# A fused four-layer transformer kernel: row maxima transposed in one rounded pass, more idle products and new interleaving tables

## The reference

```
scores = jnp.where(causal, scores, NEG)
m = jnp.max(scores, axis=-1, keepdims=True)
e = jnp.exp(scores - m)
attn = e / jnp.sum(e, axis=-1, keepdims=True)
```

## Time and profile before

| | us |
|---|---|
| median of three runs | 3338.98 |
| the profiled execution | 3332.12 |
| its span, first to last instruction | 3330.2 |
| mean granted TensorE clock in it | 0.851 |

### The profile page before, as it was taken

One profiled execution on the slowest core, in us unless ns is written; L12 is line 12 of the kernel. 1 busy time (PEld: TensorE's weight loads), 2 busy tenths in 40 slices (PEclk: granted clock), 3 DMA queues, 4 the chain that ended last, 5 costly groups with the idle time before them and its releaser, 6 DMA issues.

```text
span 3330.2 us, 50269 instructions
## 1 busy us (share of the span) xinstructions
PE 2776.6 (83%) x20640; PEld 1752.4 (53%) x20640; DVE 1760.9 (53%) x2698; ACT 1912.7 (57%) x1963; POOL 3.6 (0%) x13
## 2 busy tenths in 40 slices
PE   7999989778997789977898888987889879897426
PEld 4776556454564545645455554555545545554213
DVE  5464464644656446564555545555455554564425
ACT  2333334875248753587535864468634686347996
POOL 0000000000000000000000000000000000000000
PEclk8998899779997688977999778987779887898558
DMA  3000000000000000000000000000000000000000
GB/s 128 2 1 1 19 2 1 1 1 7 1 1 1 0 8 1 1 1 1 8 2 1 1 1 8 2 1 1 1 4 2 1 1 1 4 1 1 0 0 7
DMA packets 4570, 18.83 MB, mean 6 GB/s; under 512 B 608, under 2 KB 864, under 8 KB 3808
## 3 DMA queue, kind: packets, MB, share of 16 engines
q1 hardware_dynamic: 4320, 15.38, 1.2%
HBM read 13.28 MB, written 2.10 MB: 5 GB/s over the span
## 4 chain that ended last, share of the span: by engine, by line
PE 58%; ACT 19%; DVE 12%; issue 11%; DVEq 0%; DMA 0%; ACTq 0%; SPq 0%
ACT back_cosines L1379 6%; PE two_ps L1934 3%; ACT back_cosines L1381 3%; PE one_ps L918 2%; PE one_ps L1934 2%; PE two_ps L1334 2%; PE one_ps L1220 2%; PE two_ps L966 1%; PE one_ps L1782 1%; PE two_ps L918 1%; ACT L1379 1%; PE one_ps L893 1%; PE two_ps L613 1%; PE one_ps L899 1%; PE one_ps L822 1%
## 5 line engine op out<-in xcount | busy, mean ns | idle before, releaser
L1379 ACT ACTIVATE back_cosines<-back_cosines 128x2048 f32<-128x2048 f32 x256 | 473.3, 1899 | 0.5
L989 ACT ACTIVATE front_scratch<-one_ps 128x1152 f32<-128x1152 f32 x168 | 171.6, 1022 | 230.4 <-PE one_ps L904 230.2
L1934 PEld LDWEIGHTS two_ps<-zero_f,wts 128*128 128x128 f32 x1270 | 210.1, 232 | 114.6 <-issue 90.9
L1934 PE MATMUL two_ps<-zero_f,wts 128*128 128x128 f32 x1270 | 235.2, 327 | 35.1 <-DVE back_cosines L1452 18.1
L1381 ACT ACTIVATE back_cosines<-back_cosines,wts 128x2048 f32<-128x2048 f32 x128 | 252.1, 1994 | 13.3 <-DVE back_cosines L1452 13.1
L853 DVE TENSOR_REDUCE front_negm<-one_ps 128x8 f32<-128x1024 f32 (+1 forms) x168 | 202.5, 1221 | 99.0 <-PE one_ps L828 97.7
L1389 DVE TENSOR_REDUCE back_nsum<-back_cosines 128x8 f32<-128x2048 f32 x64 | 144.4, 2281 | 186.9 <-ACT back_cosines L1379 186.9
L752 ACT ACTIVATE back_cosines<-two_ps,wts 128x512 fp32r<-128x512 f32 x28 | 19.2, 687 | 236.3 <-PE two_ps L966 236.3
L822 PE MATMUL one_ps<-front_qkr 32*128 32x128 f32 (+1 forms) x896 | 117.8, 363 | 42.7 <-issue 34.4
L1452 DVE TENSOR_SCALAR back_cosines<-two_ps 128x2048 f32<-128x2048 f32 x56 | 128.1, 2287 | 30.2 <-PE two_ps L1313 30.1
L989 ACT ACTIVATE back_cosines<-two_ps 128x1152 f32<-128x1152 f32 (+1 forms) x84 | 86.1, 1025 | 98.3 <-PE two_ps L904 98.3
(11 more groups left out here) (635 smaller groups left out, 5941.8 us busy)
## 6 DMA issues: line engine op xcount, KB each, us to landing
wts<-w_dram SPq DMA_DIRECT2D x1, 4184.0 KB, 15.2
front_xin<-x_dram SPq DMA_DIRECT2D x8, 256.0 KB, 4.3
out_dram<-back_z SPq DMA_DIRECT2D x8, 256.0 KB, 2.0
wts<-w_dram SPq DMA_DIRECT2D x1, 1736.5 KB, 19.1
wts<-w_dram SPq DMA_DIRECT2D x1, 1199.0 KB, 5.4
wts<-w_dram SPq DMA_DIRECT2D x1, 1152.0 KB, 16.7
wts<-w_dram SPq DMA_DIRECT2D x3, 256.0 KB, 5.9
wts<-w_dram SPq DMA_DIRECT2D x1, 516.5 KB, 4.5
```

Of the source, the lines that this page charges most:

```text
L989: nc.scalar.activation(h.probs[:, e % 2, 0:n * HEADW].rearrange("p (k c) -> p k c", c=HEADW), h.ps[:, 0:n, 0:HEADW], ACT.Exp, scale=float( ...
L1379: nc.scalar.activation(cosines, cosines, func, scale=scale).then_inc(h.arc_pass.sem, 1)
L1934: nc.tensor.matmul(h.ps[:, bank, quarter * P:(quarter + 1) * P], C("ident"), zero_f[:].broadcast_to([P, P]), start=True, stop=True, skip_g ...
```

## The change

- `negm` is kept in the rounded type (F32R). The reduction itself rounds minus the maximum. The four small copies, the high part and the low part are gone, with their semaphores and constants. The neighbouring column stays zero.
- The four transpositions become products of `negm` and a rounded identity (`ident_r`), in the new `max_end_pe`. Three of them wait for all reductions but the last, the fourth for all. The first three go to bank 0, the fourth to bank 1.
- `max_end_dve` copies 128x384 when three tiles are there and 128x128 when the fourth is; a score set waits for both.
- `IDLE_WORK` has 179 products per turn of the loop instead of 119, 138 instead of 66 in "fronts" and 220 instead of 172 in "backs": 1432 in all, 480 more.
- `PE_RUNS`, `ACT_RUNS` and `DVE_RUNS` have new numbers; the number of steps in the stages has changed with the above.

```diff
-            self.negm, self.maxTr = sb("negm", [P, TILES, P]), sb("maxTr", [P, TOK], F32R)
+            self.negm, self.maxTr = sb("negm", [P, TILES, P], F32R), sb("maxTr", [P, TOK], F32R)
...
-            pe.wait_ge(h.max_pair.sem, h.max_pair.at(turn, s))
+            yield from max_end_pe(pe, h, turn, s, MSETS)
+
+        def max_end_pe(pe, h, turn, s, sets):
+            yield
+            pe.wait_ge(h.max_done.sem, h.max_done.at(turn, s, sets - 1))
             for t in range(TILES):
-                last = nc.tensor.transpose(h.ps[:, 0, t * P:(t + 1) * P], h.negm[:, t, :], C("ident"))
-            last.then_inc(h.negm_ps.sem, 1)
+                if t == TILES - 1:
+                    yield
+                    pe.wait_ge(h.max_done.sem, h.max_done.at(turn, s, sets))
+                last = nc.tensor.matmul(h.ps[:, t // (TILES - 1), t % (TILES - 1) * P:(t % (TILES - 1) + 1) * P],
+                                        h.negm[:, t, :], ident_r[:], start=True, stop=True, skip_group_check=True)
+                if t >= TILES - 2:
+                    last.then_inc(h.negm_ps.sem, 1)
...
-        def max_end_dve(dve, h, turn, s, sets):
-            yield
-            dve.wait_ge(h.max_done.sem, h.max_done.at(turn, s, sets))
-            for t in range(TILES):
-                last = nc.vector.tensor_copy(max_columns(h, slice(t, t + 1), 1)[:, 0], max_columns(h, slice(t, t + 1), 0)[:, 0])
-            last.then_inc(h.max_pair.sem, 1)
-            yield
-            dve.wait_ge(h.negm_ps.sem, h.negm_ps.at(turn, s))
-            high_dve(dve, h.ps[:, 0, :], h.high[:, 0, :], "m_sign", h.negm_high)
-            yield
-            dve.wait_ge(h.negm_high.sem, h.negm_high.at(turn, s))
-            split_dve(dve, h.ps[:, 0, :], h.high[:, 0, :], "m_low", h.maxTr[:, :], h.negm_ready)
+        def max_end_dve(dve, h, turn, s):
+            for i, columns in enumerate((slice(0, (TILES - 1) * P), slice((TILES - 1) * P, TOK))):
+                yield
+                dve.wait_ge(h.negm_ps.sem, h.negm_ps.at(turn, s, i + 1))
+                nc.vector.tensor_copy(h.maxTr[:, columns], h.ps[:, i, 0:columns.stop - columns.start]).then_inc(h.negm_ready.sem, 1)
...
 IDLE_WORK = {
     "front": {
-        1: (2, 3, (0, 0)), 2: (2, 3, (0, 0)), 3: (3, 3, (0, 0)), 4: (3, 3, (0, 0)), 5: (3, 3, (0, 0)), 9: (3, 3,
+        1: (2, 3, (0, 0)), 2: (2, 3, (0, 0)), 3: (3, 3, (0, 2)), 4: (3, 3, (0, 0)), 5: (3, 3, (3, 0)), 9: (3, 3,
```

More of the change, by code:

```diff
@@ L409, in __init__ @@
             parts = scratch[:, 8 * TOK:12 * TOK]
-            self.negm = scratch[:, 12 * TOK:13 * TOK].rearrange("p (t c) -> p t c", t=TILES)
+            self.negm = rounded("negm", [P, TILES, P], 12 * TOK)
             self.y = sb("y", [P, TOK])
@@ L465, in __init__ @@
         self.negm_clear = signal("negm_clear", {"causal2": 1})
-        self.max_pair = signal("max_pair", {s: 1 for s in CAUSAL + ("mqa",)})
-        self.negm_high = signal("negm_high", {s: 1 for s in CAUSAL + ("mqa",)})
-        self.negm_ps = signal("negm_ps", {s: 1 for s in CAUSAL + ("mqa",)})
-        self.negm_ready = signal("negm_ready", {s: 1 for s in CAUSAL + ("mqa",)})
+        self.negm_ps = signal("negm_ps", {s: 2 for s in CAUSAL + ("mqa",)})
+        self.negm_ready = signal("negm_ready", {s: 2 for s in CAUSAL + ("mqa",)})
         self.score_ps = signal("score_ps", {s: CSETS for s in CAUSAL} | {"linear": CSETS, "mqa": QSETS, "arccos": 2 * UNITS})
@@ L830, in max_pe, with max_columns @@
                 last.then_inc(h.max_ps.sem, 1)
+            yield from max_end_pe(pe, h, turn, s, MSETS)
+        def max_end_pe(pe, h, turn, s, sets):
             yield
-            pe.wait_ge(h.max_pair.sem, h.max_pair.at(turn, s))
+            pe.wait_ge(h.max_done.sem, h.max_done.at(turn, s, sets - 1))
             for t in range(TILES):
-                last = nc.tensor.transpose(h.ps[:, 0, t * P:(t + 1) * P], h.negm[:, t, :], C("ident"))
-            last.then_inc(h.negm_ps.sem, 1)
-        def max_columns(h, tiles, i):
-            return h.negm[:, tiles, :].rearrange("p t (j r) -> p t j r", r=QUAD)[:, :, :, 0:2 * GROUPS]\
-                .rearrange("p t j (g i) -> p t j g i", i=2)[:, :, :, :, i]
+                if t == TILES - 1:
[5 more added lines that the diff above has]
+                    last.then_inc(h.negm_ps.sem, 1)
+        def max_columns(h, tile):
+            return h.negm[:, tile, :].rearrange("p (j r) -> p j r", r=QUAD)[:, :, 0:2 * GROUPS]\
+                .rearrange("p j (g i) -> p j g i", i=2)[:, :, :, 0]
         def max_dve(dve, h, turn, s):
@@ L848, in max_dve @@
                 if m == 0 and not h.front:
[L849 removed]
+                    nc.vector.memset(h.negm[:].bitcast(F32), 0.0).then_inc(h.negm_clear.sem, 1)
                     dve.wait_ge(h.negm_clear.sem, h.negm_clear.at(turn, s))
                 dve.wait_ge(h.max_ps.sem, h.max_ps.at(turn, s, m + 1))
[L852 removed]
+                into = max_columns(h, 2 * b + qt)[:, js, g0:g0 + ng]
                 nc.vector.tensor_reduce(into, h.ps[:, js, :].rearrange("p j (g k) -> p j g k", k=keys),
                                         AX.X, ALU.max, negate=True).then_inc(h.max_done.sem, 1)
[L855 to L868 removed]
+            yield from max_end_dve(dve, h, turn, s)
+        def max_end_dve(dve, h, turn, s):
[3 more added lines that the diff above has]
+                nc.vector.tensor_copy(h.maxTr[:, columns], h.ps[:, i, 0:columns.stop - columns.start]).then_inc(h.negm_ready.sem, 1)
         def trio(e):
@@ L887, in causal_scores_pe @@
                         yield
-                        pe.wait_ge(h.negm_ready.sem, h.negm_ready.at(turn, s))
+                        pe.wait_ge(h.negm_ready.sem, h.negm_ready.at(turn, s, 2))
                     else:
@@ L1184, in mqa_pe @@
                         last.then_inc(h.max_ps.sem, 1)
-            yield
-            pe.wait_ge(h.max_pair.sem, h.max_pair.at(turn, s))
-            for t in range(TILES):
-                last = nc.tensor.transpose(h.ps[:, 0, t * P:(t + 1) * P], h.negm[:, t, :], C("ident"))
-            last.then_inc(h.negm_ps.sem, 1)
+            yield from max_end_pe(pe, h, turn, s, 2 * TILES)
             for e in range(QSETS + 1):
@@ L1255, in mqa_dve @@
                     dve.wait_ge(h.max_ps.sem, h.max_ps.at(turn, s, 2 * m + c + 1))
-                    nc.vector.tensor_reduce(max_columns(h, slice(m, m + 1), 0)[:, 0, js, 0], h.ps[:, js, 0:SEQ],
+                    nc.vector.tensor_reduce(max_columns(h, m)[:, js, 0], h.ps[:, js, 0:SEQ],
                                             AX.X, ALU.max, negate=True).then_inc(h.max_done.sem, 1)
-            yield from max_end_dve(dve, h, turn, s, 2 * TILES)
+            yield from max_end_dve(dve, h, turn, s)
             for b in range(PAIR):
```

15 lines of the change are left out of this document (6 added, 9 removed), and 168 rows, old and new, of tables (ACT_RUNS, DVE_RUNS, IDLE_WORK, PE_RUNS).

## The result

The changed kernel takes 3297.04 us (median of 20 runs, 3283.84 to 3339.44), the kernel before 3331.91 (20 runs beside them, 3318.77 to 3346.66). The ratio is 0.9899, 95% interval 0.9881 to 0.9916: 1.0% or some 34 us faster, where 75 were forecast.

A forecast was written before the change was run, and what follows sets the result against it. PE was taken to bound the kernel, partly at the low clock, with ACT bounding some stretches. Maxima -8 and -24, idle products +36, clock -79 sum to -75; 3332.1 gives 3257, plus 7 for the median: 3264 us, range 3190 to 3375.

The forecast's parts named there:

- Tables: New step order on PE, ACT and DVE: the real work moves little, 0 us, bounds -10 and +10.
- Idle products: 480 more, mostly at turn starts and around mqa: one in three on the path at full clock, +36 us.
- clock: Low-clock PE stretches partly return to full clock: 10 us a turn, 15 in "fronts", 4 in "backs"; -79, bounds 0 and -180.
- the wash: Rival, chance 0.12: clock returns in one or two stretches a turn; products +60, maxima -32, clock -28: 0, 3339 us.
- the slow rival: Rival, chance 0.18: waits around mqa don't raise the clock, products on the path at 0.426 us: +102 less 32, 3409 us.
- The 930 us at 1.2 GHz: Low-clock time before the change: 74 us in "fronts", 105 per turn, 230 in "backs"; not all of it costs time.
- Maxima, latency: Last reduction to end of maxima 2.5 us shorter per stage: -16 in mqa, -8 in causal, together -24, bounds 0 and -80.
- PE work -8: Rounded products replace the maxima's transpositions, 0.065 us each by the lower end: -8 us over 32 stages; other end +14.
- fill the wait: In the 24 causal stages the other half's products cover the maxima's wait: a third of a us each, -8 us.
- DVE work: Maxima copies and steps: 1.05 us less in each of 32 stages, 34 us of DVE, hidden by the other half's reductions: 0.
- What would show it: Predicted signs: 128 single records, last copy under 1 us, clock about 0.88, turn near 397 us, ACT 240, PE near 2780.
- The clock returns nearly everywhere: Rival, chance 0.12: products stand where the waits are, so clock gives -150 in place of -79: 3193 us.

The follow-up runs named there:

- The late wait: The changed kernel, but the products of all four tiles of a maximum wait for the last reduction: 3340.5 us, ratio 1.0017 to the kernel before.

## Why the forecast was too large

**The sum failed because its terms were added as if each held whatever the others are.** Its parts, each against what a run shows:

- *Tables: 0, bounds -10 and +10.* This is the step that failed most. "The real work moves little" was read off the order and priced at nothing. With the new maxima the new order costs 29 us at the old counts and gives 57 at the new ones, both far outside the bounds. Taken one after the other in the order of the sum's parts, maxima, tables, products, the runs give -9, +29 and -53, where -32, 0 and -43 were forecast. That is -33, and the tables are the largest of the three errors. In the changed kernel, the old tables and counts in "fronts" give another 14 us.
- *Idle products +36 and clock -79.* Together -43. In the new order -53 was measured, so their balance was nearly right there. In before's order it is +33 with the new maxima, which is the wash's balance (60 less 28), and +74 with the old, between the wash and the slow rival (102). The clock did rise as forecast, 0.876 for "about 0.88". The 930 us at 1.2 GHz that the forecast starts from are a little short: they take turn 2 for all six, and a mean of 0.851 makes it 990.
- *Maxima, latency -24, and PE work -8.* The path became 27 us shorter, by 2.1 us in an mqa stage and 0.4 in a causal one, so these sizes were right. What they are worth was not: 9 us in all with 952 products, 50 or 42 with 1432. The late wait shows that a wait ahead of other work is paid nearly in full (45.7 us of path for 40 of time), by the other half too, which stands behind the waiting product. I had let the other half's products "fill the wait"; they can do so only if they stand ahead of it in PE's queue.
- *PE work -8, from a product of 0.065 us.* Wrong: three products keep 0.55 us (their starts lie 0.14 apart), and their loads take 188 ns against 140 for a transposition. The rule of the Trainium skill that I weighed there ("Perfetto Trace Analysis", Optimizing Tensor Performance, Transposes) would have put the transposition ahead; here it is 13 us behind, with overlapping intervals. The other one ("TensorE: Matmul & The Clock Gate", Part 4, a transposition doesn't count as PE's activity as a product does) fits that sign; that it is the cause is not shown.
- *DVE work 0.* 1.05 us a stage was called hidden, since DVE is busy for half of a stretch. Putting back 1.4 us a stage cost 19 us. From 20 to 60 us into a turn DVE is busy for 28.7 of 40, not half.
- *What would show it.* Right: single records, copies (the two together 0.75 to 0.84 us), ACT's 240 a turn, the clock. Wrong: PE busy rose to 2838, not 2780; a turn is 399.7 and not 397, being a mean of 393 to 407; from the last reduction to the last copy it is 1.15 us in the mqa stage above, not under 1.
- *The rivals.* "The clock returns nearly everywhere" and the wash didn't come. What I had no rival for is that one part changes the sign of another, as order and products do, and a stretch that gets slower, "fronts".

What stays open: why order and products need each other, and why 1432 products make the maxima worth some five times as much. Why "fronts" is slower: in its profile PE's busy time and its idle time both grow over the whole stretch and no single wait holds them. And which event decides whether a turn keeps the clock: the same instructions go both ways in one run.

## What to carry to other kernels

Filler work, order and waits have no prices of their own: with the same maxima, the same 480 products cost 33 us in one order and gave 53 in another, so a change of several parts should be forecast (and measured) as a chain of steps, each against the last, and stretch by stretch. On an in-order queue shared by two halves, what a wait costs is what stands behind it: moved one step ahead, with the same instructions, it cost 40 us. Where the clock moves, compare repeated stretches of the same instructions within a profile first: their spread tells what the clock is worth before any experiment does. Of two kernels with the same products, set the time of each run against its clock: one that lies on the other's line lost by the clock, one above it by something else.

## What the runs showed of the hardware

- The granted clock differs between turns of identical instructions, and one stretch of 40 us makes 10 us of a turn: 395.2 with 0.96 there, 406.1 with 0.62.
- A higher clock that is bought with filler need not pay. From 0.801 to 0.851, which is 338 us less at 1.2 GHz (1328 to 990), brought no time in the kernel before, since 952 products paid for it. Among the runs of the changed kernel, where the instructions are the same, the time goes from 3318.1 at 0.864 to 3283.8 at 0.881: some 20 us for 0.01 of clock.
- The late wait is not the clock: its runs take 3332.9 and 3333.9 at 0.872, where the changed kernel takes 3296.8 and 3308.5.
- A rounded 128x128 product by the identity takes no less than a transposition of the same tile, 302 and 300 ns, with a weight load of 188 against 140 ns.
- Run to run the changed kernel spreads over 56 us and the one before over 28, so a median of 20 says more than any profile of it.
